# Semaphore clearing between six stages: its own blocks taken out, numbers kept apart, the first two stages' cleared inside the third

## The reference

```python
x = x + _L0_xattn_ref(_layernorm(x), ctx_512, ...)  # stage a: causal attention to a context
x = x + _L0_attn_ref(_layernorm(x), ...)            # stage b: gated delta rule, conv, 32 value heads
x = x + _L0_ffn_ref(_layernorm(x), ...)             # stage c: feed-forward, ternary weights, 8-bit rows
x = x + _L1_xattn_ref(_layernorm(x), ctx_512, ...)  # stage d: latent cross-attention, 16 heads
x = x + _L1_attn_ref(_layernorm(x), ...)            # stage e: causal attention, 16 heads on 4
x = x + _L1_ffn_ref(_layernorm(x), ...)             # stage f: top-2 of 8 experts, low-rank parts
```

```python
def simple_rms_norm(x):
    n = jnp.linalg.norm(x, axis=-1, keepdims=True)
    return x / jnp.maximum(n, 1e-12) * jnp.sqrt(d)
def activation_quant(x):
    scale = 127.0 / jnp.clip(jnp.max(jnp.abs(x), axis=-1, keepdims=True), EPS)
    return jnp.clip(jnp.round(x * scale), -128, 127) / scale
h = gelu(gelu(bitlinear158(x, w1)))
return bitlinear158(h, w2)
```

## Time and profile before

| | |
|---|---|
| median of 3 runs | 939.4 us (939.21 to 941.13) |
| profiled execution, its own time | 938.21 us |
| its span, first to last instruction | 936.4 us |
| TensorE busy in matmuls | 780.0 us (83%) |
| VectorE, ScalarE, GpSimd busy | 503.3, 386.8, 188.6 us |
| mean granted TensorE clock | 0.903 of 2.4 GHz |
| DMA, all queues | 53.95 MB, 58 GB/s in the mean |

### The profile page before, as it was taken

How to read it: one execution, slowest core, us unless ns; L and a number is a source line. 1 busy time by engine, 2 the same in 40 slices (tenths; PEclk the granted TensorE clock), 3 DMA queues, 4 the chain that set the end, 5 groups by cost and what they waited for, 6 DMA issues and landing times. The chain is left out here.

```text
span 936.4 us, 13981 instructions
## 1 busy us (share of the span) xinstructions
PE 780.0 (83%) x5047; PEld 609.9 (65%) x5048; DVE 503.3 (54%) x1202; ACT 386.8 (41%) x999; POOL 188.6 (20%) x376
## 2 busy tenths in 40 slices
PE   5756538999999989962369999999999958995997
PEld 4645327898898888851337666767677737773654
DVE  1525817768768762326436665566666225452561
ACT  1504764555555554324215555555555312222220
POOL 1013883156536534000000000000000000000000
PEclk9657768999999999975569999999999979997999
DMA  6005111632122111100195121212110160000000
GB/s 221 1 0 195 61 29 45 244 101 79 41 86 81 39 41 54 27 1 0 35 237 166 19 38 20 37 20 37 20 26 6 13 240 31 1 1 1 0 1 11
DMA packets 49123, 53.95 MB, mean 58 GB/s; under 512 B 33856, under 2 KB 38976, under 8 KB 47808
## 3 DMA queue, kind: packets, MB, share of 16 engines
q1 hardware_dynamic: 47776, 50.95, 17.8%
q0 software_dynamic: 1280, 2.12, 2.3%
HBM read 51.69 MB, written 1.36 MB: 57 GB/s over the span
## 5 line engine op out<-in xcount | busy, mean ns | idle before, releaser
L1531 ACT COPY d_Pt<-bank 128x512 f32<-128x512 f32 x96 | 51.7, 589 | 101.8 <-PE bank L1454 101.8
L1606 DVE TENSOR_REDUCE d_nm<-scores 128x1 f32<-128x1024 f32 x64 | 75.5, 1220 | 20.4 <-PE scores L1447 20.4
L1010 DVE SCALAR_TENSOR_TENSOR b_yc<-b_cpad,b_slab,b_yc 128x256 f32<-128x256 f32 x192 | 79.4, 487 | 0.0
L1543 ACT ACTIVATE d_Pr<-scores,d_negm 128x1024 f32<-128x1024 f32 x64 | 70.8, 1110 | 17.7 <-DVE d_negm L1609 17.7
L1454 PEld LDWEIGHTS bank<-cst,d_Pr 128*128 128x128 f32 x512 | 56.2, 141 | 29.4 <-issue 24.7
L1454 PE MATMUL bank<-cst,d_Pr 128*128 128x128 f32 x512 | 69.2, 278 | 0.7 <-DVE d_Pt L1583 0.4
L1447 PE MATMUL scores<-d_KM,d_Q 64*128 64x512 f32 x256 | 65.4, 630 | 2.0 <-ACT d_Q L1522 2.0
L1467 PE MATMUL bank<-d_Pt,d_KV 128*64 128x128 f32 x1024 | 63.0, 276 | 0.0
L647 PE MATMUL bank<-xnT,b_slab 128*128 128x256 f32 x256 | 60.9, 387 | 2.3 <-ACT b_cpad L870 2.3
L1467 PEld LDWEIGHTS bank<-d_Pt,d_KV 128*64 128x64 f32 x1024 | 55.2, 137 | 7.8 <-issue 5.8
L647 PEld LDWEIGHTS bank<-xnT,b_slab 128*128 128x128 f32 x256 | 48.4, 196 | 9.1 <-issue 2.9
(11 more groups left out here) (326 smaller groups left out, 1655.2 us busy)
## 6 DMA issues: line engine op xcount, KB each, us to landing
b_slab<-in_b_slab SPq DMA_DIRECT2D x16, 520.0 KB, 4.7
b_wz<-in_b_wz SPq DMA_DIRECT2D x16, 256.0 KB, 3.0
b_wo<-in_b_wo SPq DMA_DIRECT2D x16, 256.0 KB, 4.3
d_w<-in_d_w SPq DMA_DIRECT2D x16, 224.0 KB, 2.4
b_DT<-b_cs SPq DMA_DIRECT2D x2, 1536.0 KB, 10.1
f_w<-in_f_w SPq DMA_DIRECT2D x3, 896.0 KB, 10.8
c_w<-in_c_w SPq DMA_DIRECT2D x2, 1024.0 KB, 6.4
d_wo<-in_d_wo SPq DMA_DIRECT2D x1, 2048.0 KB, 8.2
```

The source lines that it names most:

```text
L1010: last = dve.scalar_tensor_tensor(yc[x][:, ch], src, tap, yc[x][:, ch], ALU.mult, ALU.add)
L1531: act.copy(Pt[g][:].rearrange("p j q -> p (j q)"), TP[g % 2]).then_inc(pt_cp[g % 2], 1)
L1543: act.activation(Pr[b][:, keys], scores[:, 2 * k:2 * k + 2, :].rearrange("p g k -> p (g k)"), ACT.Exp, bias=negm[:, b:b + 1], accum_out=su ...
L1606: last = dve.tensor_reduce(nm2[:, b, k:k + 1], scores[:, 2 * k:2 * k + 2, :].rearrange("p g k -> p (g k)"), AX, ALU.max, negate=True)
```

## The change

The block after each stage is gone, and with it one of the two barriers of each stage's end. The stages no longer reuse the numbers of the one before: the semaphores of stages a and b are entered in an `ExitStack` called `first`, those of c to f in `rest`. The numbers of `first` are given back ahead of stage e, where `early_f` and stages e and f take them again; so they have to be zero by then. GpSimd clears them, all 73, inside stage c's block, between `rstd` and its wait for `ss_done`. The semaphores of stages c to f are no longer cleared in the program at all.

```diff
+        first, rest = ctx.enter_context(ExitStack()), ctx.enter_context(ExitStack())
+        env["used"] = []
         for n, st in enumerate(stages):
+            if n == 2:
+                env["spent"], env["used"] = env["used"], []
             if n == 3:
                 bc.close()
                 env["w_e"] = early_e(a, sb_kept, sem)
             if n == 4:
+                first.close()
                 env["w_f"] = early_f(a, sb_kept, sem)
+            env["sems"] = first if n < 2 else rest
             with ExitStack() as own:
-                env["used"] = []
                 st(nc, a, env, own)
-
-                with nc.Block() as block:
-                    @block.vector
-                    def _(dve):
-                        for used in env["used"]:
-                            dve.sem_clear(used)
...
     def sem(name):
-        env["used"].append(own.enter_context(nc.semaphore("c_" + name)))
+        env["used"].append(env["sems"].enter_context(nc.semaphore("c_" + name)))
         return env["used"][-1]
...
         def _(pool):
             env["ln_gpsimd"](2)
+            for spent in env["spent"]:
+                pool.sem_clear(spent)
             pool.wait_ge(ss_done, 1)
```

More of the change, by code:

```diff
@@ L226, in sem @@
     def sem(name):
-        env["used"].append(own.enter_context(nc.semaphore("a_" + name)))
+        env["used"].append(env["sems"].enter_context(nc.semaphore("a_" + name)))
         return env["used"][-1]
@@ L428, in sem @@
     def sem(name):
-        env["used"].append(own.enter_context(nc.semaphore("b_" + name)))
+        env["used"].append(env["sems"].enter_context(nc.semaphore("b_" + name)))
         return env["used"][-1]
@@ L1332, in sem @@
     def sem(name):
-        env["used"].append(own.enter_context(nc.semaphore("d_" + name)))
+        env["used"].append(env["sems"].enter_context(nc.semaphore("d_" + name)))
         return env["used"][-1]
@@ L1663, in sem @@
     def sem(name):
-        env["used"].append(own.enter_context(nc.semaphore("e_" + name)))
+        env["used"].append(env["sems"].enter_context(nc.semaphore("e_" + name)))
         return env["used"][-1]
@@ L1903, in sem @@
     def sem(name):
-        env["used"].append(own.enter_context(nc.semaphore("f_" + name)))
+        env["used"].append(env["sems"].enter_context(nc.semaphore("f_" + name)))
         return env["used"][-1]
```

## The result

The changed kernel took 925.1 us in the median of five executions, four of them between 920.7 and 926.6, against 939.4 us before. The ratio is 0.984, with a 95% interval of 0.9815 to 0.9869, so 14.8 us less, between 12.3 and 17.4. A second set on another occasion gave 924.0 us and 0.984 (0.9815 to 0.9865). The forecast was 923.0 us in a range of 921 to 926. The fifth execution took 1635 us; it is left out of the ratio (without it the median is 925.0 us), nothing like it came in any of the later sets, and its cause was not found.

What follows compares the result with a forecast made beforehand. The prediction took the barriers at the six stage ends, where all engines stop, as the bound. Clearing blocks (15.7 us) and TensorE's clock (0.7) came off 939.4, giving 923.0 us, ratio 0.983, range 921.0 to 926.0.

Steps and rivals of the forecast that it cites:

- The blocks that go, 15.7 us: At the six stage ends: removing the clearing blocks saves 15.7 us, summed from the differences between two releases.
- the second rival: GpSimd's clears in stage c cost 102 ns each, 1.7 to 2.4 us late: 924.7 to 925.4 us; chance 0.08.
- The second way: Cross-check of the clearing blocks: 162 clears at 83 ns plus six barriers at 0.3 us give 15.3 us.
- What could be late next: nothing taken off: Across the stages: transfers start earlier with their stage, so no late DMA takes the gain back; 0 us.
- The first rival: Something late, a transfer or the clock, takes back 3 to 5 us: 926 to 929 us; chance 0.05.
- The 73 clears on GpSimd, 67 ns, hidden: Stage c, ahead of `c_rn`: clears take 4.9 us, fit the room of 5.7 or 5.04 us, delay nothing.
- The bound from the two semaphore rows: GpSimd's clear price scaled by semaphore events, 17 ns there against 21 on VectorE: 67 ns each.
- third rivals: GpSimd's clears cost like computing instructions, 0.38 us each, 22.0 us beyond the room: 945.7 us, slower; chance 0.02.
- The rule that spoke against it: GpSimd's sequencer passes instructions to eight cores with software lookup, so a clear might cost like a small GpSimd operation.
- TensorE's clock, 0.7 us: Stage d's start: a shorter wait may keep the clock at 2.4 GHz for 16 transposes; 0.7 us, bounds 0 and 1.4.
- the prediction's own sign of being wrong: Stage d's start: transposes still taking 3.5 us as before, which would put the time at 923.7 us.
- the fourth rival: A second barrier remains at the stage ends or the clears' time reappears there: 925 to 939 us; chance 0.03.

Runs made afterwards that it cites:

- before_ranges: Kernel before, clearing blocks and both barriers kept, with one clear per run of neighbouring numbers, 8 instead of 162: 923.4 us, ratio 0.985.
- clears_at_end_of_c: Changed kernel with GpSimd's 73 clears moved behind its last `c_rn` in stage c: 925.7 us, 0.984 of the kernel before.
- clears_twice: Changed kernel with each of GpSimd's 73 clears given twice, 146 in all: 926.6 us, 0.987 of the kernel before.
- after_again: The changed kernel, unaltered, timed once more beside the kernel before on the same chip: 924.0 us, ratio 0.984.
- before_spread: Kernel before, all six clearing blocks kept, with stage e's 18 weight loads given out one to three at a time during stage d: 940.9 us, ratio 1.001.
- e_weights_later: Changed kernel with stage e's weight loads issued behind the `d_w` loads of heads 2 and 3 instead of ahead: 926.9 us, 0.989 of the kernel before.
- e_weights_spread: Changed kernel with stage e's 18 weight loads given out one to three at a time ahead of heads 4 to 14's `d_w` loads: 918.3 us, ratio 0.976.

## Why the prediction was right, step by step

*The blocks that go, 15.7 us.* Right in mechanism and size. The stage table gives the 15.7 us as the whole of the clearing blocks, and nothing of it came back as another wait at the stage ends. The ratios of both sets, 0.984, are 14.8 and 15.0 us. The trace sets this apart from the rivals, the time does not: 925.1 us of the first set lies within the second rival's 924.7 to 925.4 as well as within the forecast's bounds. The second way, 83 ns a clear and 0.3 us a barrier, is confirmed by before_ranges: with 154 clears fewer 12.3 us went (80 ns each), with the barriers kept.

*What could be late next: nothing taken off.* Wrong in one place. The argument was that everything in a stage moves forward together, and looked for transfers at the stage starts only. Stage d's transfers do start with it, but in the changed kernel TensorE comes to head 2 at 37.6 to 39.5 us after the release, before the weights are there. The first rival named this kind of loss, at 3 to 5 us; it measured 0.2 to 1.9 us of waiting in the seven profiles that show it, and stage d, at 288.1 to 290.2 us, stayed near before's 288.6 in all of them.

*The 73 clears on GpSimd, 67 ns, hidden.* Right: 72 ns from one to the next, 5.3 us in all, in the longer room of 5.7 us, since the queue hands them out while `rstd` runs. The bound from the two semaphore rows was 5 ns low, that from VectorE 11 ns high. clears_at_end_of_c shows the cost to be nothing, clears_twice that the slack ends where the prediction put it and that lateness passes on one for one. The second and third rivals fell with the 72 ns; the second's 102 ns was not quite GpSimd's shortest operation, since two memsets of the same line took 99 ns.

The rule that spoke against it (the Trainium skill, GPSIMD Engine Reference, section 2.1 Instruction dispatch) doesn't bear on a clear: it is recorded on GpSimd's queue at 44 ns, below its shortest computing operation of the earlier trace rows, and runs beside one.

*TensorE's clock, 0.7 us.* The mechanism was right for the start, the term wrong for the stage. The prediction took half because the clock's level would depend on where its rise near the end of stage c falls, and so it came out: of ten profiles with the wait of 1.65 us six began warm, 1.94 us for the transposes, 1.6 less than before and more than the upper bound of 1.4 (which rested on 2.1 us for the 16 transposes, where the row of four gives only 2.5), and four began cold, 3.3 to 3.7 us. One of the four is after_again's: that is the prediction's own sign of being wrong, transposes as slow as before, which was to give 923.7 us. This execution took 926.1 us, with the slower stage e; the median of its set was 924.0. But even where the start was warm it was not worth anything: stage d was 288.1 to 290.2 us long with warm starts and 288.8 to 289.0 with cold ones, against 288.6 before. The step that failed is the silent one, that what is won at a stage's start is won at its end: head 2's product had to wait for its weights in both. With the loads spread the same start is worth 1.3 to 1.4 us (286.6 and 286.7 warm, 288.0 cold). before_spread is the other half, no gain from that edit with a cold start; it is one profile.

*The sum.* 939.4 - 15.7 is 923.7, and without the clock term the two sets lie 0.3 and 1.4 us above it (924.0 and 925.1 us). That one execution of the kernel had 920.7 us and another 926.1 is stage e, for which the prediction counted nothing: the same program took 100.2 or 105.8 us for that stage. The bounds missed this source of scatter: the range of 921 to 926 held both medians, but four of the ten single executions lie outside it (919.2, 920.7, 926.1 and 926.6 us), so that both medians fell inside is in part luck. The prediction's own chances put 0.90 on the two cases that the range holds, not 0.88.

*No change in what it does:* the blocks are gone in the trace, as the lists said, so the fourth rival fell.

## What to carry to other kernels

The price of housekeeping at a barrier is read between the two releases, not from the recorded length of its instructions: 54 ns were recorded where 83 were paid, and all engines paid. Before moving such instructions to an idle engine, try to have fewer of them, since one clear of a range did in 0.4 us what 55 did in 4.5. And when a stage is made to start earlier or faster, look for the first transfer that the next head or tile needs and ask what stands ahead of it in the queue: here weights that are needed over 250 us later stood there, and moving them all at once only found the next victim, while giving them out one by one took a further 5 to 7 us, of which that stage accounts for 0.8 to 2.1 between profiles with like starts, and for 3.6 only against the first profile. And read more than one profile of a kernel before explaining a stage that changed by 1 or 2 us: the first profile here had a stage d of 290.2 us, the others 288.1 to 289.0.

## What the runs showed of the hardware

- A clear of one semaphore is paid at 83 ns on VectorE's queue and at 72 ns on GpSimd's (recorded as 54 and 44). A clear of a range took 375 ns for 55 numbers on VectorE and 438 ns for 73 on GpSimd.
- Such instructions run ahead beside a computing instruction of the same engine: GpSimd's began as `rstd` began, and VectorE's as a 1.23 us quantisation did.
- The granted clock of TensorE can fall while it is busy: in after_again it stood at 2.4 GHz from 754.7 us on, ran into a gap of 0.9 us (755.2 to 756.1), and was back at 1.2 GHz from 758.2 to 765. It fell once more from 771.8 to 775.2. The same program with an earlier rise and without these falls was 5.6 us faster in the stage. The Trainium skill, TensorE: Matmul & The Clock Gate, section HAM oscillation, ties such relapses to waits for data between stretches of work; here one short gap stood there in both executions, and only one of them had the relapse.
- The level of the clock at the start of stage d was not decided by the gap of 1.65 us ahead of it: behind that gap the same 16 transposes took 1.94 us in six profiles and 3.3 to 3.7 us in four, by whether the clock had risen 0.8 to 1.3 us before the release or stood at its lower rate then.
- A one-kilobyte transfer of GpSimd, 3.3 us to landing in the median of the profile before, was waited for 9.9 us at its worst in e_weights_later (3.2 us at most in e_weights_spread), while stage e's weights were being issued from SyncE's queue.
